# Second-slot units on other PSUM bank pairs, and the first logits ahead of the last unit, in one block of a language-model tower

## The reference, cut to what matters

```
logits1 = xg @ phi.T                          # 32 groups of 64 rows, 128 slots (8 experts x 16)
disp1   = softmax(logits1, over the rows)
comb1   = softmax(logits1, over the slots)
slots   = disp1.T @ xg
yn      = l2norm(slots) * scale * gamma2
means   = mean of yn over the 4 neighbouring slots
se2     = l2norm(means @ w_slot2) * scale     # the "second slots"
logits2 = yn @ se2.T                          # inside each expert
disp2   = softmax(logits2, over its rows)
comb2   = softmax(logits2, over its columns)
slots2  = disp2.T @ yn
out     = experts(slots2), mixed back by comb2 and comb1
```

## Time and profile before

| | us |
|---|---|
| median of three runs | 542.17 (540.88 to 544.49) |
| the profiled execution | 544.31 |
| its span in the trace | 542.5 |
| first level, units and second level | about 273 to 397 |
| stretch from the last fillers to the first inputs | 317.9 to 355.8 |
| experts and the end | 397.9 to 542.5 |

### The profile page before, as it was taken

The page is one execution under the profiler, slowest core; times in us unless marked ns, Lnnn a source line. Parts: engine busy times, 40 slices in busy tenths (PEclk is TensorE's granted clock), DMA queues, the critical chain, the costliest instruction groups (busy, mean ns, idle before and its releaser), DMA issues. The chain is left out here.

```text
span 542.5 us, 13583 instructions
## 1 busy us (share of the span) xinstructions
PE 514.5 (95%) x5421; PEld 422.2 (78%) x5421; DVE 315.8 (58%) x743; ACT 252.8 (47%) x823; POOL 103.1 (19%) x189
## 2 busy tenths in 40 slices
PE   6999999999999999999978899899989999999996
PEld 5888888965565566666867664588889999999985
DVE  3348679677767767755227866577723444434443
ACT  1244343456566567644347658757732322323220
POOL 6380000021042144041223760000100000000000
PEclk9999999999999999999989999899999999999999
DMA  6190000000000000000074000600059999899733
GB/s 246 29 316 3 2 0 1 2 1 1 1 1 2 1 1 1 2 2 1 1 306 160 2 2 2 234 1 2 1 221 408 314 359 383 319 325 310 196 53 123
DMA packets 20722, 58.80 MB, mean 108 GB/s; under 512 B 3042, under 2 KB 9796, under 8 KB 20548
## 3 DMA queue, kind: packets, MB, share of 16 engines
q1 hardware_dynamic: 14756, 49.47, 24.7%
q0 software_dynamic: 1056, 4.33, 4.2%
q10 hardware_dynamic: 4848, 4.13, 2.6%
HBM read 53.21 MB, written 4.33 MB: 106 GB/s over the span
## 5 line engine op out<-in xcount | busy, mean ns | idle before, releaser
L1152 DVE TENSOR_REDUCE qk<-banks 128x4 f32<-128x1024 f32 x48 | 58.8, 1225 | 39.5 <-PE banks L615 39.5
L2092 PE MATMUL banks<-slots_t,w 64*128 64x128 f32 x1344 | 80.7, 272 | 1.1 <-PEq L1323 1.1
L2092 PEld LDWEIGHTS banks<-slots_t,w 64*128 64x128 f32 x1344 | 79.1, 188 | 1.5 <-issue 1.3
L615 PE MATMUL banks<-qk_t 16*128 16x256 f32 x384 | 54.4, 400 | 2.6 <-DVE qk L1152 2.4
L622 PE MATMUL banks<-qk_t 17*128 17x256 f32 x384 | 54.4, 400 | 0.0
L615 PEld LDWEIGHTS banks<-qk_t 16*128 16x128 f32 x384 | 33.2, 184 | 20.3 <-issue 13.7
L2195 DVE TENSOR_REDUCE tokens<-banks 128x192 f32<-128x384 f32 x32 | 17.8, 557 | 47.2 <-PE banks L2123 47.2
L931 ACT ACTIVATE wk_t<-banks 128x512 f32<-128x512 f32 x48 | 26.1, 595 | 32.8 <-PE banks L622 32.8
L355 POOL TENSOR_TENSOR qk<-qk,att_rms 128x384 f32<-128x384 f32 x14 | 11.4, 837 | 150.6 <-ACT att_rms L903 150.6
L2165 ACT ACTIVATE yn_t<-banks,b_sb 128x128 f32<-128x128 f32 x64 | 18.3, 368 | 45.3 <-PE banks L2092 45.3
L2165 ACT ACTIVATE tokens<-banks,b_sb 128x128 f32<-128x128 f32 x64 | 18.3, 369 | 44.7 <-PE banks L2092 44.7
(11 more groups left out here) (251 smaller groups left out, 1128.6 us busy)
## 6 DMA issues: line engine op xcount, KB each, us to landing
w<-in_w SPq DMA_DIRECT2D x28, 768.0 KB, 10.6
w<-in_w2e SPq DMA_DIRECT2D x24, 384.0 KB, 11.9
yn_t<-in_w SPq DMA_DIRECT2D x4, 768.0 KB, 10.3
yn_t<-in_w2e SPq DMA_DIRECT2D x8, 384.0 KB, 12.5
rows_scratch<-tokens ACTq DMA_DIRECT2D x28, 96.0 KB, 7.5
yn_all<-rows_scratch POOLq DMA_DIRECT2D x7, 384.0 KB, 9.8
w<-in_w_slot SPq DMA_DIRECT2D x4, 576.0 KB, 8.9
w_slot<-in_w_slot SPq DMA_DIRECT2D x3, 576.0 KB, 5.7
```

The costliest lines, as they stand in the source:

```text
L615: last_best = nc.tensor.matmul(g.ps[MAXES[hh]][:, half * SEQ:(half + 1) * SEQ], g.qk_t[bn_ % 2][row:row + HDIM, bq, 0, half * P:(half + 1) ...
L1152: nc.vector.tensor_reduce(to, flat(MAXES[0], MAXES[1] + 1).rearrange("p (h t n) -> p h t n", h=2, n=SEQ), AX.X, ALU.max, negate=True).then ...
L2092: return nc.tensor.matmul(bank[:, j * P:(j + 1) * P], g.w1[n % BUFS][rows, first + j * P:first + (j + 1) * P], x, start=start, stop=stop, ...
```

## The change

It touches only `slots_and_dispatch`.

- The unit pairs `MADE` become 2, 6, 2, 6, 0, 2, 6, 2, and the turned units go to banks 4 and 5. The second level's banks move too: logits 0 and 1, turned logits 6, turned dispatch 2, weights 7, inputs 4 and 5.
- On TensorE `make_se2(1)` stands ahead of `turn_last`, with waits for the banks 6 and 7 (`comb_kept`, `rest_kept`) in place of the wait for `slots_normed`. The fillers ahead of it go from 16 to 6.
- On TensorE `make_logits(0)` stands ahead of `make_se2(7)`, and `make_logits(1)` ahead of `turn_se2(7)`.
- On ScalarE both last copies of units move one step ahead of `row_exp(0)` and `col_exp(0)`. On VectorE `mask(0)` stands ahead of `norm_se2(7)` as before, with the loop written otherwise, and `mask(1)` comes ahead of the last unit's copies.
- The waits on banks follow the new numbers.

```diff
-        MADE = (2, 4, 2, 4, 0, 2, 4, 0)
-        SE2_TURN = (6, 7)
+        MADE = (2, 6, 2, 6, 0, 2, 6, 2)
+        SE2_TURN = (4, 5)
...
-        LOGITS, COLUMNS, DISP, WEIGHTS, INPUTS = (2, 3), 4, 0, 5, (6, 7)
+        LOGITS, COLUMNS, DISP, WEIGHTS, INPUTS = (0, 1), 6, 2, 7, (4, 5)
...
                 if u == 1:
-                    pe.wait_ge(F["slots_normed"], GPS * BATCH)
+                    pe.wait_ge(F["comb_kept"], BATCH)
+                    pe.wait_ge(F["rest_kept"], BATCH - 1)
...
                 if u > PAIRED:
-                    pe.wait_ge(S["normed"], u - 2)
+                    pe.wait_ge(S["normed"], u - 2 if u < UNITS - 1 else UNITS - 2)
...
                 if k == 0:
-                    pe.wait_ge(F["rest_kept"], BATCH - 1)
-                    pe.wait_ge(F["comb_kept"], BATCH)
+                    pe.wait_ge(F["slots_normed"], GPS * BATCH)
...
                     pe.wait_ge(S["kept_s"], 4 * PAIRED)
-                    pe.wait_ge(S["normed"], UNITS - 2)
+                    pe.wait_ge(S["normed"], PAIRED + 1)
...
-            keep_busy(nc, g, 1, 16)
+            keep_busy(nc, g, 1, 6)
+            make_se2(1)
             turn_last(BATCH - 1)
-            make_se2(1)
             for u in range(2, UNITS):
+                if u == UNITS - 1:
+                    make_logits(0)
                 make_se2(u)
                 turn_se2(u - 2)
-            make_logits(0)
             turn_se2(UNITS - 2)
             turn_logits(0)
+            make_logits(1)
             turn_se2(UNITS - 1)
             for n in range(1, BATCH):
-                make_logits(n)
+                if n > 1:
+                    make_logits(n)
...
+            keep_se2(UNITS - 2)
             row_exp(0)
-            keep_se2(UNITS - 2)
+            keep_se2(UNITS - 1)
             col_exp(0)
-            keep_se2(UNITS - 1)
...
-            for u in range(2, UNITS - 1):
+            for u in range(2, UNITS):
+                if u == UNITS - 1:
+                    mask(0)
                 norm_se2(u)
                 keep_se2(u - 1)
-            mask(0)
-            norm_se2(UNITS - 1)
-            keep_se2(UNITS - 2)
             col_max(0)
             invert_row(0)
+            mask(1)
             keep_se2(UNITS - 1)
             dispatch(0)
             for n in range(1, BATCH):
-                mask(n)
+                if n > 1:
+                    mask(n)
```

## The result

| | us |
|---|---|
| before, median of 7 runs | 542.17 (540.88 to 544.49) |
| with the change, median of 7 runs | 544.22 (543.24 to 545.84) |
| ratio after to before | 1.0043, 95% interval 1.0024 to 1.0063 |
| forecast | 543.2, from 540.3 to 545.2 |
| span and time of the profiled execution after | 541.5 and 543.33 |

The profiled execution after is itself faster than the one before (541.5 against 542.5), so spans of single executions mislead here. The medians decide.

What follows compares the result with a forecast made beforehand. The prediction took TensorE, busy for 95% of the span, as the bound. Its terms, -1.43 (order) + 1.39 + 1.0 (two clock falls) = +1.0, added to the median 542.17 gave 543.2 us, range 540.3 to 545.2.

Steps and rivals of the forecast that it cites:

- The front: TensorE before unit 2: ten fewer fillers start it 2.23 us earlier, with 0 to 0.3 us lost to ScalarE.
- The chain of 2.98 us at the end of the units: From unit 7's products to `turn_se2(6)`: ScalarE's chain stays 2.98 us, so the start is only 0.60 us earlier.
- The fillers' time: Rival: the end of the units follows TensorE, so all 2.23 us arrive, giving 539.9 us; chance 0.04.
- ScalarE's order and `turn_disp(0)`: End of the units: column exponentials behind unit 7's copies put `turn_disp(0)` at 353.04, against 353.08 before at an even clock.
- The clock: TensorE's two new waits, 2.0 and about 3.1 us, each lower its clock: first fall 1.0 us (0 to 1.4), second 1.39.
- carrying the difference to the median: Final sum: the +1.0 us worked out against the profiled execution is added to the median of 542.17.
- the gain of 1.43: At `turn_disp(0)`: 353.04 instead of 354.47, there only if TensorE's clock doesn't fall.
- the three likely cases: Whole time: two falls 543.2 us (chance 0.45), a single fall 542.2 (0.30), no fall 540.8 (0.10).
- a ScalarE that falls behind: Rival: ScalarE loses more than its 0.57 us margin at unit 2, giving some 544.6 us; chance 0.06.
- Unit 1 ran ahead: Rival denied this: unit 1 needs something later than 319.25, the 2.23 us are lost, at most 545.4 us; chance 0.05.
- A clock that holds: Rival: neither new wait at the end of the units lowers TensorE's clock, giving 540.8 us; chance 0.10.
- One fall: Rival: the wait of 2.0 us passes at the high clock and only the second lowers it, 542.2 us; chance 0.30.

Runs made afterwards that it cites:

- the second profile: The changed kernel timed again with no edit: 544.63 us, ratio 1.0027 to the kernel before.
- the front alone: Kernel before with the new banks, 6 fillers and unit 1 ahead of `turn_last`, its whole end in the old order: 541.11 us, ratio 0.9999.
- the new banks alone: Kernel before with only the new bank numbers, 16 fillers and every step in the old order: 541.53 us, ratio 1.0008.

## Why the prediction was right, and what it mis-sized

**The front.** Right: ten fillers gave 2.09 (unit 2's start) and 2.08 (the stretch) of the 2.23, inside the 0 to 0.3 allowed for losses, and ScalarE kept up.

**The chain of 2.98 us at the end of the units.** Right: unit 7's products end at 341.20 - 316.58 = 24.62 from the first filler (342.48 - 317.91 = 24.57 was worked out), and `turn_se2(6)` starts at 27.59, where 345.46 - 317.91 = 27.55 was worked out, after a wait of 1.88 for the 2.0 forecast. The fillers' time could not arrive whole. Putting the logits back removed the wait, which shows its cause.

**ScalarE's order and `turn_disp(0)`.** Right: 35.10 measured, 353.04 - 317.91 = 35.13 worked out, after waits of 0.49 and 2.29 where 2.5 to 3.1 was said; and the claim that both orders are equal at an even clock holds within 0.02 us (35.10 and 35.09, stretches 78.62 and 78.60). This is what made the sign right, since the two profiles alone show `turn_disp(0)` 1.46 us earlier.

**The clock.** The mechanism was right, the two terms in it were off. In the first profile after, the first wait was passed at the full clock (term 1.0 between 0 and 1.4, measured 0 there and 1.67, above the upper bound, in the second profile). The second fall cost 81.10 - 78.62 = 2.48 instead of 1.39, since the clock stayed down for about 7 us. Why it lasted longer than in the kernel before is not shown. That TensorE was idle when it began doesn't explain it: the short fall of the kernel before also began in the wait (at about 349.7, from the 0.84 in the earlier trace rows, with work from 349.91), and the long one of the front alone began after the wait (at about 348.3, from the 0.83 above, with work from 347.12). That the two terms add up to 2.39, near to 2.48, is luck.

**The step that failed in size: carrying the difference to the median.** The prediction measured against an execution before that had a fall in the stretch, costing 1.42 (80.02 against 78.60), and gave the median the same difference: 542.17 + 1.0. But most executions of the kernel before have no fall at all, 68 of 90, so its median pays little or nothing of this. Fillers in its wait took 0.5 us off the median, with 1 inside the interval of the ratio. The changed kernel had at least one fall in 16 of its 19 executions, and filling both waits took 2.9 us off the median (544.63 to 541.70). The difference, 2.9 - 0.5 = 2.4, agrees with what was measured (2.3 from the first ratio), as far as such medians tell. In the terms of the sum: the gain of 1.43 was 1.39 of the profiled execution's own fall and 0.04 of order. Without that fall the sum is 0 + 1.39 + 1.0 = 2.4, and 542.17 + 2.4 = 544.6, where 544.22 and 544.63 were measured; that its two terms for the clock make up for each other is the luck named above.

**The range.** It held the 544.22, but not through the three likely cases, which ended at 543.2. Its upper part was there for a ScalarE that falls behind, and that did not happen. That it covered the larger price of the clock is luck.

**The rivals.** Unit 1 ran ahead and ScalarE kept up, so these two fall. A clock that holds happened in 3 of 19 executions; they lie at a median of 541.43, level with the kernel before, and not at 540.8. One fall (542.2) was priced too low for the same reason: the three executions with a mean clock of 0.996 or 0.997 took 542.77, 543.24 and 543.96.

The Trainium skill ("TensorE: Matmul & The Clock Gate", section "Why this matters for your kernels") asks for no idle time above about 3 us if the clock is to hold. These runs disagree: filling a wait of 2.35 us with 2.0 us of products, in the front alone, moved the ratio to the kernel before from 0.9999 to 0.9950 and the falls from 11 of 12 executions to 0 of 9, and the low clock came during or after waits of 1.89 and 2.35. The Trainium skill ("TensorE: Matmul & The Clock Gate", section "What's actually happening") says that the point at which the clock changes is not tied to the kernel's start and varies between runs. The trace agrees: around the same wait of 1.75 us at 273, ahead of all that the change touches, the clock was 0.82 in the profile before and 1.00 in the profile after.

## What to carry to other kernels

Before moving work ahead, see what it was filling: the logits cost nothing while they stood in ScalarE's chain of 2.98 us, and cost 1.54 of their 1.63 us ahead of it. First work the order out row by row with every row at the full clock, as the prediction did, then look at each wait of TensorE that is left. A fall of the clock behind it can cost as much as the new order saves, and a few throwaway products in the wait are cheap to try. The waits needn't have grown: the front alone kept the old ones and lost most of its 2.08 us to the clock. And before carrying a difference from one profile to the median, compare the profiled execution's mean clock (0.994 here) with that of the other executions of the same kernel (mostly 1.00).

## What the runs showed of the hardware

The same wait is followed by the lower clock in some executions and not in others: 2.34 us without a fall with the new banks alone, 2.35 with one in the kernel before and in the front alone. How often it falls is not a matter of the wait's length alone: with the same waits, 2 of 11 executions had a fall with the new banks alone and 11 of 12 with the new front; why is open. A low stretch cost 1.42 us of TensorE's time in the kernel before, where it lasted some 3.4 us, and 2.48 and 2.95 (79.47 against 76.52 for the front) where it lasted some 7 us. It can begin during the wait (kernel before, changed kernel) or over a microsecond after work resumed (front alone; changed kernel, second profile). Products whose result nobody reads held the clock in these profiles: none of the five with a filled wait ahead of `turn_disp(0)` or `turn_se2(7)` shows a fall behind it, and 6 of the 51 executions of these five kernels had a fall anywhere.
